# New order of all engines' steps, moved PSUM banks, and maxima split by the upper halves of float32, in a decoder layer

## The reference

```python
x = x + attn(layernorm(x), W_qkv, W_out)         # 16 heads of 16, causal softmax
x = x + xattn(layernorm(x), ctx_2048, mask)      # softmax(x ctx^T / 16) ctx over 64 masked context rows
x = x + ffn(layernorm(x), gate_w, down_w, ...)   # both products as "bit linear"
# bit_linear(x, w, g): xn = rms_norm(x, g); scale = 127 / max|xn|
#   activations: round(xn * scale) / scale; weights: clip(round(w / mean|w|), -1, 1) * mean|w|
# ffn: gate, up = bit_linear(x, gate_w) (704 columns each); bit_linear(gate * sigmoid(gate) * up, down_w)
```

## Time and profile before

| | us |
|---|---|
| median of 3 runs (lowest, highest) | 219.57 (218.81, 221.8) |
| the profiled execution | 218.97 |
| its span, first to last instruction | 216.9 |
| TensorE busy | 193.8 (89%) |
| VectorE busy | 173.0 (80%) |
| ScalarE busy | 150.5 (69%) |
| GpSimd busy | 135.6 (63%) |

### The profile page before, as it was taken

How to read it: one execution, slowest core, us unless ns; L and a number is a source line. 1 busy time by engine, 2 the same in 40 slices (tenths; PEclk the granted TensorE clock), 3 DMA queues, 4 the chain that set the end, 5 groups by cost and what they waited for, 6 DMA issues and landing times. The chain is left out here.

```text
span 216.9 us, 10902 instructions
## 1 busy us (share of the span) xinstructions
PE 193.8 (89%) x4095; PEld 149.9 (69%) x4099; DVE 173.0 (80%) x555; ACT 150.5 (69%) x422; POOL 135.6 (63%) x290
## 2 busy tenths in 40 slices
PE   4989998999899898999999999998999979987773
PEld 4777776878587666878787868686878755533431
DVE  1234589879896879999897988997989989999771
ACT  3469756767678686888787887888778665675631
POOL 6400326466836675667686658678577668989980
PEclk9999999999999999999999999999999999999999
DMA  6999000101010102020101011010101102000011
GB/s 176 381 328 335 10 5 5 48 8 48 6 50 30 50 3 76 2 66 7 47 29 53 21 34 40 28 46 26 48 26 50 41 32 66 14 0 16 13 48 48
DMA packets 11474, 12.79 MB, mean 59 GB/s; under 512 B 1009, under 2 KB 10801, under 8 KB 11442
## 3 DMA queue, kind: packets, MB, share of 16 engines
q1 hardware_dynamic: 11442, 12.41, 17.9%
HBM read 10.31 MB, written 2.10 MB: 57 GB/s over the span
## 5 line engine op out<-in xcount | busy, mean ns | idle before, releaser
L2031 POOL TENSOR_TENSOR zh<-hh,gd 128x352 f32<-128x352 f32 x32 | 30.3, 953 | 6.4 <-DVE hh L1336 5.7
L331 PE MATMUL ps<-yaT,wqk 128*128 128x128 f32 x256 | 31.7, 277 | 1.1 <-ACT yaT L683 1.1
L331 PEld LDWEIGHTS ps<-yaT,wqk 128*128 128x128 f32 x256 | 30.1, 193 | 2.0 <-ACT yaT L683 1.7
L1201 DVE TENSOR_REDUCE mx<-ps 128x16 f32<-128x1024 f32 x16 | 19.5, 1220 | 7.3 <-PE ps L367 7.3
L315 PE MATMUL ps<-wg,zT 128*128 128x352 bf16 x128 | 22.5, 313 | 0.8 <-ACT zT L683 0.5
L1947 POOL TENSOR_TENSOR rs<-ve,neghalf 128x1 f32<-128x1 f32 x32 | 20.3, 633 | 2.7
L788 ACT ACTIVATE th_sb<-ps,th 128x352 f32<-128x352 f32 x32 | 17.4, 553 | 6.0 <-PE ps L315 2.9
L683 ACT ACTIVATE hT<-ps 128x256 bf16<-128x256 bf16 (+1 forms) x32 | 15.1, 490 | 6.4 <-PE ps L309 6.4
L740 ACT ACTIVATE pT<-ps 128x512 f32<-128x512 f32 x32 | 18.1, 597 | 2.2 <-PE ps L404 1.7
L1945 POOL TENSOR_SCALAR ve<-mv 128x1 f32<-128x1 f32 x32 | 7.0, 219 | 19.3 <-issue 11.8
L2053 POOL TENSOR_SCALAR hq<-zh,qh 128x704 f32<-128x704 f32 x16 | 13.6, 848 | 8.7 <-DVE qh L1365 8.4
(11 more groups left out here) (123 smaller groups left out, 522.6 us busy)
## 6 DMA issues: line engine op xcount, KB each, us to landing
ct_in<-ctx_t SPq DMA_DIRECT2D x16, 128.0 KB, 2.1
cn_in<-ctx_n SPq DMA_DIRECT2D x16, 128.0 KB, 2.2
out<-o_out SPq DMA_DIRECT2D x16, 128.0 KB, 1.7
wg<-gate_t SPq DMA_DIRECT2D x1, 1408.0 KB, 7.8
x_in<-x SPq DMA_DIRECT2D x1, 1024.0 KB, 11.1
wd<-down_t SPq DMA_DIRECT2D x1, 640.0 KB, 8.4
wqk<-wqkv_t SPq DMA_DIRECT2D x1, 512.0 KB, 4.5
x_in<-x SPq DMA_DIRECT2D x1, 512.0 KB, 9.8
```

Of the source, the lines that this page charges most:

```text
L331: last = pe.matmul(qk_ps[:, e * P:(e + 1) * P], wqk[:, c, e * P:(e + 1) * P], yaT[:, t % 2, c, :], start=(c == 0), stop=(c == DC - 1))
L1201: V.tensor_reduce(out=mx[:, t % 2, :, :], in_=scores, op=ALU.max, axis=AX).then_inc(ev["mx_d"], 1)
L2031: G.tensor_tensor(zh[:, t % 2, part], hh[:, t % 2, part], gd[:, part], ALU.mult).then_inc(ev[f"zh_d{j}"], 1)
```

## The change

It has four parts.

1. The split of the maxima. The maxima now lie in one float32 tensor `mx` with room for eight terms. The upper 16 bits of a float32 are themselves a bfloat16 (cut, not rounded), so no cast is made: `mx_halves[..., 1]` reads them in place. `max_hi` and `max_mid` are gone; `max_rest` and `max_lo` subtract the upper halves. `transpose_max` reads every second 16-bit element.
2. PSUM banks. The transpose of oN moves to bank 3, that of yx to bank 0, the result of `down` to bank 2, the weight totals to bank 6. The waits in TensorE's list follow.
3. The lists of all engines are in another order, the loop's `step(s)` among them. One store and one load of SyncE change places.
4. `keep_busy` can wait for readers, and there are 43 of these products in the drain instead of 35, 25 of them in two runs of 8 and 12 and one of 5.

```diff
-         mx = sb("mx", [P, 2, 4, 4])
-         mrest = sb("mrest", [P, 2, 4, 4])
-         mh = sb("mh", [P, 2, 4, TERMS, 4], BF16)
+         mx = sb("mx", [P, 2, 4, TERMS, 4])
+         mx_halves = mx[:, :, :, :, :].bitcast(BF16).rearrange("p s g r (h w) -> p s g r h w", w=2)
...
-         oT_ps = bank(0, D)
+         oT_ps = bank(3, D)
-         yxT_ps = bank(1, D)
+         yxT_ps = bank(0, D)
-         d_ps = bank(0, D)
-         wtot_ps = bank(3, 2)
+         d_ps = bank(2, D)
+         wtot_ps = bank(6, 2)
...
+            def less_upper(t, r, done):
+                V.tensor_tensor(mx[:, t % 2, :, r + 1, :], mx[:, t % 2, :, r, :], mx_halves[:, t % 2, :, r, :, 1],
+                                ALU.subtract).then_inc(ev[done], 1)
...
-            def keep_busy(k, count):
+            def keep_busy(k, count, *users):
+                freed(users)
...
             def step(s):
-                readout(s - 1, ("q_d", s + 1), ("k0_d", s + 1), ("k1_d", s + 1))
+                readout(s - 1, ("q_d", s + 1), ("k0_d", s + 1), ("k1_d", s + 1), ("out_d", s - 5))
+                cross_readout(s - 3, ("pxT_d", s - 2))
                 transpose_ya(s + 1, ("zT_d", s - 3))
-                cross_readout(s - 3, ("pxT_d", s - 2))
...
-                transpose_yx(s - 2, ("v_d", s + 1))
-                transpose_readout(s - 1, ("yaT_d", s + 2))
+                transpose_yx(s - 2, ("yaT_d", s + 2))
+                transpose_readout(s - 1, ("x2_d", s - 2))
...
-                down(s - 5, ("hT_d0", s - 4))
+                project_v(s + 1, ("expx_d", s - 1))
                 transpose_cross_weights(s - 2, ("x1_d", s))
-                project_v(s + 1, ("expx_d", s - 1))
+                down(s - 5, ("q_d", s + 2), ("k0_d", s + 2), ("k1_d", s + 2))
+                transpose_z(s - 3, ("hT_d0", s - 4))
                 scores_q(s + 1, ("exp_d0", s + 1), ("exp_d1", s + 1))
-                transpose_z(s - 3, ("out_d", s - 4))
...
```

More of the change, by code:

```diff
@@ L1933, in _ @@
             scale_qh(15)
+            integers_h(14)
+            residual_3(13)
+            integers_h(15)
             residual_3(14)
-            integers_h(15)
             residual_3(15)
```

1176 lines of the change are left out of this document (566 added, 610 removed).

## The result

The changed kernel takes 211.36 us (median of four runs, 211.24 to 214.57) beside 219.37 us for the kernel before (218.81 to 221.8). The ratio is 0.9625, with an interval of 0.9547 to 0.9704. It was timed twice more in other sets of runs: 212.2 us at 0.9683 (0.9644 to 0.9722), and 211.54 us at 0.9651 (0.9623 to 0.9679). The change makes the kernel 7 to 8 us faster. I had predicted 215.6 us, 4.0 less than before, with a range from 211.5 to 220.5: the direction was right, the gain was half of what came, and 211.36 lies just under the range.

What follows compares the result with a forecast made beforehand. TensorE was taken to bound the loop, then VectorE and GpSimd, then a chain of single steps. Terms -0.3 - 2.8 - 0.25 - 0.65 = -4.0 us gave 215.6 us against the median 219.57, range 211.5 to 220.5.

Steps and rivals of the forecast that it cites:

- The first tiles: Stretch before the loop: swaps other than scores_k(0) could move it either way by about 1 us, costed at nothing.
- `scores_k(0)` first: First tiles on TensorE: scores_k(0) ahead of project_v(1) starts up to 0.6 us earlier, net -0.3 us.
- The loop: Nine steps from project_qk(6) to project_qk(15): half of the 5.6 us over a floor of 10.72 us a step goes, -2.8.
- The casts: VectorE, 32 casts dropped: 0.07 us each, 0.14 a loop step, worth only what VectorE's lateness costs TensorE.
- Bank 2 and bank 3 cost nothing: Loop on TensorE: new waits for residual_3 (bank 2) and residual_2 (bank 3) cost nothing, or a few tenths for bank 3.
- The slower rival: Loop: bank 2 ties TensorE to VectorE, a step takes 11.9 us, +5.0, total 223.4 us; chance 0.10.
- The drain up to x2(15): Drain: two conversions behind residual_2(15) and two casts gone give at most -0.9 us; GpSimd's queue sets the pace, -0.25 taken.
- The tail: Last steps: zh halves of tile 15 together, round_h(15) 0.95 us earlier, down(14) between transposes costs 0.3; net -0.65 us.
- Unread products: Drain on TensorE: eight more ahead of transpose_z(15) cost nothing, up to +1.7 us if z came early.
- The waits are only exchanged: Rival: loop stays at 11.35 us a step, only start, drain and tail gain, 218.4 us; chance 0.20.
- Everything fits: Rival: loop reaches its floor (-5.6) and GpSimd follows x2 of tile 15 (-0.9), 212.1 us; chance 0.18.
- What would show it: Signs in the changed profile: project_qk(15) near 160 us, last down some 4 us earlier; wrong if loop takes 101 or more.

Runs made afterwards that it cites:

- e3: The changed kernel with the two casts back (old split of the maxima), all orders and banks new: 214.43 us, ratio 0.9779.
- e13: The changed kernel with normalise_x of tiles 4 to 7 moved ahead again on ScalarE, to their places before the change: 212.15 us, ratio 0.9675.
- e2: The kernel before, with its own lists and banks, but with the new split of the maxima: 218.43 us, ratio 0.9967.
- e14: The changed kernel once more with no edit, profiled without the early TensorE stall: 211.54 us, ratio 0.9651.
- e9: The changed kernel with integers_h(12) and integers_z(14) put back ahead of residual_2(15) on VectorE: 212.61 us, ratio 0.9687.
- e6: The changed kernel with all engines' old lists for the first tiles, new lists after, new banks except the weight totals' (bank 3): 228.58 us, ratio 1.0422.
- e8: The changed kernel with the four engines' old lists behind tile 15's gate_up, 14 unread products there: 213.76 us, ratio 0.9739.
- e7: The changed kernel without the 43 unread products of the drain: 216.16 us, ratio 0.9815.
- e12: The changed kernel with scores_q(2) moved back behind readout(1) and project_v(2) on TensorE: 212.52 us, ratio 0.9703.

## Why the prediction was right or wrong, by its own steps

**The first tiles, "cost at nothing": wrong, and the largest error.** I wrote that the stretch has 3.45 us of TensorE idle and that the other swaps can move it by 1 us either way. They removed 2.4 of 2.97 us of idle time between `project_qk(2)` and `project_qk(6)`, and the stretch fell by 3.56. Its rows were in the trace and I had read only their sum. e3 has 2.9 of it with the old split, so it is the order's. One swap is priced, 0.57 us (e13). The rest is not attributed: the waits for zb, 1.2 us, and for the maxima, 0.3, went too, but no experiment brings them back alone, and 1.17 us is busy time.

**`scores_k(0)` first, -0.3.** It does start earlier, 14.14 - 11.47 = 2.67 us behind `project_qk(1)` in place of 3.19, but from `project_qk(1)` to `project_qk(2)` it takes 7.22 us, before 7.18. Nothing gained. The 1.08 us ahead of `project_qk(2)` came from elsewhere: 0.2 is the start, 0.23 a shorter `project_qk(0)` (2.28 to 2.05 us; both vary from trace to trace, the second up to 2.86), and the rest a wait of `project_qk(1)` for its transposed input, 0.62 us before, which is gone.

**The loop, -2.8: mis-sized, measured -0.9.** Two things failed in it. The excess of 5.6 us over the floor was taken from one step of 10.72, the lightest; the busy time in the earlier trace rows, 97.78 of 102.1, gave the right excess, 4.3, in the row above. And of the 1.75 us that I had placed, 0.74 was the loop's jump, of which there are four whatever the order, 2.16 us in all; I had seen that it waited for nothing and still let half of such times go. The 1.01 us wait ahead of the transpose of yx did go. The other 2.16 us fell by 1.74, more than the half that I took, and the four jumps grew by 0.87, which I had not considered; with that the loop gained 0.90. The first two steps took 12.28 and 12.41 us before and 11.12 and 11.80 after; the seven behind them take 0.9 us more than before.

**The casts, 0.07 us each: within the bounds, but near their middle.** VectorE in the loop fell from 88.70 to 85.91 us, by 2.79 for the whole of nine steps, of which e2 shows 2.26 for the split alone, 0.25 a step. That is 0.13 a cast, between 0.07 and 0.21, and so it is over the kernel (173.0 to 168.9 us in e2, for 32 casts); the 0.14 us a step that I took was too low. "Worth only what VectorE's lateness costs TensorE" held in the strict sense: nothing in the old order, 1.6 us in the new one. That the two parts of the change need each other I had not considered.

**Bank 2 and bank 3 cost nothing: right with the new lists.** In e14 TensorE has no wait of 0.2 us or more in the loop for o_out or x2 (e9 has one of 0.22). The slower rival (0.10) is wrong. With the old order at the start bank 3 costs 1.82 and 0.75 us (e6).

**The drain up to x2(15), -0.25: wrong, measured -2.58.** My bounds were 0 and -0.9, from the length of the two moved instructions. That length was read rightly: in the kernel before they waited for nothing. The step that failed is "GpSimd has the same work as before: its queue, not x2, was late", which had the right engine and the wrong conclusion. The queue was late because of its order, and the change moved `rstd_x1(14)` up in it; undone, that costs 2.1. `residual_2(14)`, ahead of the two conversions, is already 2.75 us earlier, so this gain is not theirs. With VectorE that much earlier they would wait for `round_h(12)`, and left in their old place they would lose 1.98 us of it at `residual_2(15)` (e9): the move keeps the gain, it doesn't make it. I had compared VectorE's list and GpSimd's last ten rows, not GpSimd's list 20 us earlier.

**The tail, -0.65: wrong by its own sum, measured +0.6.** From `inner_1(15)` to the last `down` the kernel takes 205.41 - 197.45 = 7.96 us, before 7.35. All of the drain's 2.39 us is there at `residual_2(15)` already (2.58). Yet the new tail keeps it: `inner_1(15)` stands ahead of `inner_largest(14)` now, and with the old tail behind the same `residual_2(15)` the last `down` comes 1.8 us later (e8). zh of tile 15 and `round_h`, on which I spent the working, follow in the order predicted, but not with its sizes:

```profile
197.81 1.82 POOL L1994 TENSOR_TENSOR zh<-hh,gd 128x352 f32<-128x352 f32 x2
199.62 0.37 POOL L2007 TENSOR_SCALAR m<-sqs,ek 128x1 f32<-128x1 f32 x1
200.08 0.56 POOL L2011 TENSOR_TENSOR bh<-m,neghalf 128x1 f32<-128x1 f32 x1
200.74 0.85 POOL L2016 TENSOR_SCALAR hq<-zh,qh 128x704 f32<-128x704 f32 x1
201.57 0.62 POOL L1979 TENSOR_SCALAR fd<-hm,wmean 128x1 f32<-128x1 f32 x1
202.17 0.84 POOL L2016 TENSOR_SCALAR hq<-zh,qh 128x704 f32<-128x704 f32 x1
```

Counted from the start of `inner_1(15)`, both halves of zh are done 2.18 us behind it, before 2.67: 0.5 us gained, not 1.2, since now both wait for GpSimd's steps of tile 14, where before the first half was already done. From the end of bh to `round_h(15)` it is 1.53 us, before 0.86: 0.7 us lost, not 0.25, since `scale_fd(14)` took 0.62 us and not the 0.26 that I took for it. So `round_h(15)` starts 0.2 us later and not 0.95 earlier, and from its end to the last `down` it takes 2.4 us in place of 1.96, where I had 0.3 more.

**Unread products, nothing:** no sign of a cost for the eight more, though no run takes these alone; see e7 for what all are worth. "Nothing to win there", said of the clock, holds for the kernel before; with the old 14 in the new tail e8 loses some 0.6 us to it.

**The rivals.** "The waits are only exchanged" was half right of the loop (1.74 us of waits went, 0.87 came at the turns) and wrong of the rest. "Everything fits", 212.1, gave nearly the time, and by the wrong account: it had 5.6 us in the loop, and the loop gave 0.9. Two errors, the loop too high and the ends too low, made 215.6 look closer than its reasons were.

**What would show it.** The last `down` is 213.34 - 205.41 = 7.9 us earlier, not 4. `project_qk(15)` starts at 157.96, near the 160 named, but by way of the first tiles. No cast of 128x16 is left, and VectorE's busy time fell by 7.3 us. The loop's last steps take 11.48 and 11.17 us, not 10.7 to 11. The 1.01 us wait is gone, the 0.74 is not. The drain did not grow (51.0 us, before 53.4). The loop took 101.21 us, over the 101 that I had set as the sign of being wrong, and so it was.

## What to carry to other kernels

When a change rewrites the order of several engines, look at every stretch with idle time on the engine that leads, the first tiles above all, and read each wait there by its releaser. A sum of idle time costed at nothing is a term left out. An instruction that moves is worth what it waits for in its new surroundings as well as what it does, and on a queue that is nearly full its place decides more than its length. Don't take the floor of a repeated step from its shortest instance: take the busy time of all. And the lists of engines are one object: half of one order with half of another was slower than both. When one move is changed back to price it, look whether the wait that comes is one that the old kernel had: in e12 it was not.
